# Decoder layer on one core: gathers of the expert blocks released one by one, the token picks looked up six blocks earlier, part of the last weighing and normalising moved

## What is computed

```python
logits = flat @ gate_w.T
probs = softmax(logits)
_, top_idx = top_k(logits + expert_bias, 2)
top_w = take_along_axis(probs, top_idx); top_w = top_w / top_w.sum(-1)
out = sum_e combine[:, e] * swiglu(flat, w_gate[e], w_up[e], w_down[e])    # 16 experts, width 176
out = out + swiglu(flat, sw_gate, sw_up, sw_down)                          # shared expert
x = layernorm(x + out)
```

## Time and profile before

| | us |
|---|---|
| median of 3 runs | 665.21 (661.70 to 668.49) |
| the profiled execution | 668.49 |
| its span | 666.7 |
| TensorE busy | 634.4 (95%) |
| expert blocks, first gate_up to last down | about 577 to 649 |
| rows of the routed experts, weighing, last norm | about 638 to 666.7 |

### The profile page before, as it was taken

How to read it: one execution, slowest core, us unless ns; L and a number is a source line. 1 busy time by engine, 2 the same in 40 slices (tenths; PEclk the granted TensorE clock), 3 DMA queues, 4 the chain that set the end, 5 groups by cost and what they waited for, 6 DMA issues and landing times.

```text
span 666.7 us, 12041 instructions
## 1 busy us (share of the span) xinstructions
PE 634.4 (95%) x3545; PEld 493.7 (74%) x3545; DVE 532.3 (80%) x852; ACT 455.3 (68%) x742; POOL 476.4 (71%) x456
## 2 busy tenths in 40 slices
PE   7989999999999999999999999999999999899980
PEld 6677888878888888788888887878888877555540
DVE  6999999999999999999999999958952646522345
ACT  3768788797887978878879788776423454433454
POOL 4295989879888798798987987596924644855454
PEclk9989999999999999999999999999999988999995
DMA  4261112111131121211311212042063493368444
GB/s 161 83 257 50 64 49 111 63 48 63 48 111 63 48 92 55 74 63 48 111 63 48 69 50 103 0 128 101 16 161 86 111 301 151 110 184 273 124 116 147
DMA packets 25994, 66.67 MB, mean 100 GB/s; under 512 B 4099, under 2 KB 16899, under 8 KB 23179
## 3 DMA queue, kind: packets, MB, share of 16 engines
q1 hardware_dynamic: 23131, 58.54, 26.1%
q0 software_dynamic: 2832, 7.75, 4.5%
HBM read 58.00 MB, written 9.85 MB: 102 GB/s over the span
## 4 chain that ended last, share of the span: by engine, by line
PE 82%; DVE 7%; ACT 3%; POOL 3%; issue 3%; DMA 2%; SPq 0%; ACTq 0%; DVEq 0%
PE ps L878 37%; PE ps L892 9%; PE ps L908 7%; PE ps L893 4%; PE ps L1172 4%; PE ps L810 3%; PE ps L828 3%; DVE conv L1727 3%; PE ps L1221 3%; PE ps L852 2%; DMA xb<-x_scratch,y_all 1%; PE ps L917 1%; PE ps L918 1%; POOL conv L668 1%; PE ps L1146 1%
## 5 line engine op out<-in xcount | busy, mean ns | idle before, releaser
L1727 DVE SCALAR_TENSOR_TENSOR conv<-ps,w_raw,conv 128x506 f32<-128x506 f32 (+3 forms) x352 | 320.7, 934 | 15.9 <-ACT conv L1372 9.9
L878 PE MATMUL ps<-x_hi,w_hi 128*128 128x512 f32 x384 | 158.7, 413 | 3.2 <-DVE x_lo L1648 2.1
L1372 ACT ACTIVATE conv<-ps,w_raw 128x512 f32<-128x512 f32 x160 | 108.2, 687 | 66.0 <-PE ps L878 65.5
L878 PE MATMUL ps<-x_hi,w_lo 128*128 128x512 f32 x384 | 151.6, 395 | 0.0
L878 PE MATMUL ps<-x_lo,w_hi 128*128 128x512 f32 x384 | 150.4, 392 | 0.0
L525 POOL TENSOR_TENSOR decay<-cum_b,cum_tok 128x512 f32<-128x512 f32 (+1 forms) x128 | 103.3, 828 | 8.9 <-DMA cum_b<-cum_scratch 8.9
L878 PEld LDWEIGHTS ps<-x_hi,w_hi 128*128 128x128 f32 x384 | 72.6, 189 | 21.2 <-issue 2.4
L531 POOL TENSOR_TENSOR decay<-decay,mask 128x512 f32<-128x512 f32 x64 | 82.7, 1292 | 5.0
L878 PEld LDWEIGHTS ps<-x_hi,w_lo 128*128 128x128 f32 x384 | 72.3, 188 | 17.0 <-DVE w_lo L1653 0.2
L878 PEld LDWEIGHTS ps<-x_lo,w_hi 128*128 128x128 f32 x384 | 72.7, 189 | 12.7
L1357 ACT ACTIVATE conv<-conv 128x1024 f32<-128x1024 f32 x80 | 79.3, 1059 | 1.5 <-DVE conv L1727 1.5
(11 more groups left out here) (285 smaller groups left out, 1109.8 us busy)
## 6 DMA issues: line engine op xcount, KB each, us to landing
cum_b<-cum_scratch SPq DMA_DIRECT2D x16, 1024.0 KB, 4.6
w_raw<-in_winT SPq DMA_DIRECT2D x15, 778.0 KB, 4.2
y_all<-in_wgu SPq DMA_DIRECT2D x4, 1408.0 KB, 11.9
late<-in_wdn SPq DMA_DIRECT2D x2, 1408.0 KB
x_scratch<-conv SPq DMA_DIRECT2D x19, 128.0 KB, 4.9
late<-in_woutT SPq DMA_DIRECT2D x1, 2048.0 KB, 8.2
ys_scratch<-y_blk SPq DMA_DIRECT2D x32, 64.0 KB
res_scratch<-conv SPq DMA_DIRECT2D x11, 130.0 KB
```

The costliest lines, as they stand in the source:

```text
L878: mm = pe.matmul(ps[:, tile_bank(n, tile) + hf, :], wp[:, par, w], xp[:, kk, t], start=(i == 0), stop=(i == 5))
L1372: act.activation(conv[:, par, tile, hf * 512:(hf + 1) * 512], ps[:, tile_bank(n, tile) + hf, :], ACT.Copy, scale=w_raw[:, par, tap:tap + 1 ...
L1727: dve.scalar_tensor_tensor(out=o[:, :, s:], in0=u[:, :, 0:T - s], scalar=w_raw[:, par, c:c + 1], in1=o[:, :, s:], op0=ALU.mult, op1=ALU.ad ...
```

## The change

`AHEAD` goes from 4 to 3, and each gather_block(j) with j of 3 or more waits for `tx_done` of block j-3, that is for the transpose that read the rows three blocks earlier. The pairs are gone: gather_res(b) follows gather_block(7+b) directly, with a wait on `gu_done` of the last shared item ahead of the first. `SEEN_AT` goes to item 22 (block 11), `PICK_AT` to item 25 (block 14). `beside_blocks` now spaces all rows: rows 0 and 1 wait for gate_up of block 19, rows 2 and 3 of block 20, rows 4 and 5 of block 21, rows 6 to 8 of block 22, rows 9 to 11 of block 23, rows 12 to 15 for down(33). VectorE does weigh_low of output blocks 0 to 2 ahead of gate_block(33) and weigh_high of blocks 0 and 1 ahead of gate_block(34). The last norm is done by ScalarE for blocks 0 to 3, by GpSimd for blocks 4 and 5 (after its last row gather), and by VectorE for blocks 6 and 7 after all weighing.

```diff
-SEEN_AT = TBS + 17
-PICK_AT = TBS + 18
-LAST_ACT = 5
+SEEN_AT = TBS + 11
+PICK_AT = TBS + 14
+LAST_ACT, LAST_POOL = 4, 6
+BESIDE = 19
-AHEAD = 4
+AHEAD = 3
@@ SP, output stores
                 if b < LAST_ACT:
                     sp.wait_ge(S["n2a"], b + 1)
+                elif b < LAST_POOL:
+                    sp.wait_ge(S["n2p"], b - LAST_ACT + 1)
                 else:
-                    sp.wait_ge(S["n2"], b - LAST_ACT + 1)
+                    sp.wait_ge(S["n2"], b - LAST_POOL + 1)
@@ POOL
             def gather_block(j):
+                if j >= AHEAD:
+                    pool.wait_ge(S["tx_done"], j - AHEAD + 1)
                 pool.indirect_dma_start(xb[:, j % NX, :], None, x2_dram,
...
                 if b == 0:
                     pool.wait_ge(S["st_res"], 16 * TBS)
+                    pool.wait_ge(S["gu_done"], TBS)
...
-            for j in range(AHEAD):
+            for j in range(NBLK):
                 gather_block(j)
                 if j == 2:
                     gate_shared(TBS - 1)
                     add_residual(TBS - 5)
                 elif j == 3:
                     add_residual(TBS - 4)
-            for j in range(AHEAD, NBLK, 2):
-                i = TBS + j - AHEAD
-                in_pair(i, 0)
-                gather_block(j)
-                if j == AHEAD:
+                elif j == 4:
                     add_residual(TBS - 3)
-                elif j // 2 - AHEAD // 2 <= TB:
-                    in_pair(i, 1)
-                    gather_res(j // 2 - AHEAD // 2 - 1)
-                in_pair(i, 2)
-                gather_block(j + 1)
-                if j == AHEAD:
+                elif j == 5:
                     add_residual(TBS - 2)
                     add_residual(TBS - 1)
+                if 7 <= j < 7 + TB:
+                    gather_res(j - 7)
             def beside_blocks(n):
-                if n < 6:
-                    in_pair(ITEMS - AHEAD + n // 3 * 2, n % 3)
+                j = BESIDE + min(n // 2, (n + 3) // 3)
+                if j < NBLK:
+                    pool.wait_ge(S["gu_done"], TBS + j + 1)
+                else:
+                    pool.wait_ge(S["dn_done"], ITEMS - 1)
...
+            for b in range(LAST_ACT, LAST_POOL):
+                pool.wait_ge(S["q2"], b + 1)
+                pool.tensor_scalar(o_tok[:, b, :], y_of[:, 0, b, :], ln_m2[:, b, 0:1], ln_v2[:, 1, b:b + 1],
+                                   ALU.subtract, ALU.mult).then_inc(S["n2p"], 1)
@@ DVE
             for i in range(TBS, ITEMS):
+                if i == ITEMS - 2:
+                    for b in range(HOISTED):
+                        weigh_low(b)
+                if i == ITEMS - 1:
+                    for b in range(LEADING):
+                        weigh_high(b)
                 gate_block(i)
...
-            for b in range(HOISTED):
-                weigh_low(b)
-            for b in range(LEADING):
-                weigh_high(b)
             for b in range(HOISTED, TB):
                 weigh_low(b)
             for b in range(LEADING, TB):
                 weigh_high(b)
-                if b > LAST_ACT:
-                    last_norm(b - 1)
-            last_norm(TB - 1)
+            for b in range(LAST_POOL, TB):
+                last_norm(b)
```

More of the change, by code:

```diff
@@ L274, in build_layer @@
                  "ld_sh ld_gu ld_dn ld_copy st_x2 st_res ld_res a_el "
-                 "tx_done a_xt gu_done a_s a_u p_h v_h ht_done a_ht v_ht dn_done a_y p_res v_mix st_out y_seen v_blk v_lb ys_set n2a")
+                 "tx_done a_xt gu_done a_s a_u p_h v_h ht_done a_ht v_ht dn_done a_y p_res v_mix st_out y_seen v_blk v_lb ys_set n2a n2p")
         S = {n: sem(n) for n in names.split()}
```

## The result

| | before | after |
|---|---|---|
| median, same chip, nine runs each | 662.57 us (660.66 to 668.49) | 667.59 us (665.45 to 669.90) |
| after to before | | 1.0066, 95% interval 1.0038 to 1.0095 |
| profiled execution, its span | 668.49, 666.7 | 666.86, 665.1 |

So the change costs 0.66% here, 4 to 5 us; 659.8 was forecast. The two profiled executions hide it: that of before was the slowest of its nine, and its first gather of a block starts at 573.17 us, that of after at 566.72. From there the end is 93.5 us away before (666.7 less 573.17) and 98.4 after: 4.9 more.

A forecast was written before the change was run, and what follows sets the result against it. TensorE was taken to bound the block loop, then POOL's row gathers the end. Span 666.7 less 661.35 gave 5.35 us, 1.0 from the loop; from 665.21 the same 5.4 led to 659.8, range 655.5 to 666.0.

The forecast's parts named there:

- AHEAD in the context FFN: Context FFN: position 3 gains a wait for two transposed blocks, already there in time; cost 0.
- Gathers behind tx_done: Block loop: gather(j) may start after turn_block(j-3), removing the loss at block 13; -0.63 us, bounds 0 and -0.8.
- Picks looked up earlier: Block loop, items 30 to 32: wait of 0.56 us shrinks to 0.2; -0.36 us, up to +1.5 if landing is late.
- Rows started earlier: POOL's row gathers: row 5 issued at 641.1, not 645.94; row 15 at 653.75, 5.0 us ahead.
- Weighing inside the loop: VectorE ahead of gate_block(33) and gate_block(34): the latter 0.9 us late, but covered.
- The last norm: Program's end: GpSimd norms blocks 4 and 5, 1.22 us each, delaying the output stores; costs 0.3 us.
- The base: Whole kernel: median of before taken as 665.21 us, from three runs of 661.7 to 668.49.
- (c): Blocks 6 to 23: gathers right behind turn_block cost 0.43 us per block; 2.3 slower, 667.5 us; chance 0.12.
- (a): Rows held by data, not POOL: stores land in 5 us, row 5 1.9 later; 661.7 us; chance 0.18 with (d).
- (d): Early look at the picks stalls VectorE, landing after 613.4: up to +1.5, 661.3 us; chance 0.18 with (a).

The follow-up runs named there:

- Loop alone: Kernel before with after's gathers, gather_res, AHEAD and early look at the picks, but before's tail: 661.29, 661.68, 660.95, 661.26 and 662.11 us in five runs.
- tail alone: Kernel before with after's rows, weighing, last norm and stores, but before's paired gathers, AHEAD 4 and late look at the picks: 662.71 us, ratio 1.0011.
- the kernel with the late look and no norm on GpSimd: After with gather_res in every other block only, look at the picks at items 28 and 29, no norm on GpSimd: 660.50 and 660.41 us.

## Why the prediction was wrong, step by step

After's end is 10.2 us later than forecast (98.4 against 88.2 from the first gather). The steps that failed are two. The sum has no term for late semaphores of TensorE, and the stalls that they make are 8.2 of it (98.4 against 90.2 on the clean occasion). And it prices the last norm on GpSimd at 0.3, which is the other 2.0 (90.2 against 88.2). The starts of the last gate_up and of rows 5 and 15 came out within 0.4 on a clean occasion; the base, from three runs, was 2.6 too high.

From the first gather of a block, in us. "Clean" is after on its third occasion; the last column is after without GpSimd's norms (its second run).

| | before | forecast | after | after, clean | no norm |
|---|---|---|---|---|---|
| last gate_up starts | 70.2 | 69.2 | 72.5 | 69.3 | 69.8 |
| row 5 starts | 72.8 | 67.9 | 70.8 | 67.5 | 68.0 |
| row 15 starts | 85.6 | 80.6 | 85.0 | 80.4 | 80.9 |
| end | 93.5 | 88.2 | 98.4 | 90.2 | 89.2 |

- **AHEAD in the context FFN**: cost 0, as forecast; the gathers go out 1.25 us apart in after too.
- **Gathers behind tx_done**: right on a clean occasion. Where before waits for gather(13) the period is 2.79 and not 3.42: the 0.63 are gained. They depend on the landing: without the norm, in its second run, gather(14) took 7.3 us to land, and a period there is 2.94. On an occasion with stalls this part was never run alone.
- **Picks looked up earlier**: right in place and nearly in size. The two periods with the table loads (2.90 and 3.36 before) became 2.90 and 3.10: 0.26 gained, 0.36 forecast.
- **Rows started earlier**: right to 0.4 us on a clean occasion. It needs both halves of the change. Loop alone starts row 0 at 62.3 to 65.2, tail alone at 64.25, both together at 60.4. Loop alone gains 0.6 to 1.9 us in five timings; the kernel with the late look and no norm on GpSimd gains 2.3 in two; tail alone gains nothing, but its norms are on GpSimd and cost it time at the barrier; everything but the norms gains 4.2 and 5.2.
- **Weighing inside the loop**: covered, as forecast; the last periods are 2.79 and 2.55 as before.
- **The last norm**: this step failed, and would have on any occasion. "So this costs 0.3" counted the stores alone. GpSimd is not through when its last instruction ends. Its DRAIN at the barrier ends 4.90 to 4.92 us later in all twenty traces, whether that last instruction is a norm, a small sum or the issue of a row's gather, and ScalarE's and VectorE's 0.03 to 0.05 later. In before GpSimd's last gather ends at 659.74 and its DRAIN at 664.64, ahead of SP, which comes to the barrier at 666.5; so it is hidden. With the norm the DRAIN is last, and the span ends 5.15 us behind the norm in after, in both repeats of it and in the tail alone. With the norm SP waits 2.2 us at the barrier; without it, 0.2. In time: 659.51 against 657.47 on the same occasion, 2.0 us; with stalls 667.27 against 663.36, 3.9 us, two small sums standing in for the norms. The contention with VectorE, which the Trainium skill's rule made me weigh (GPSIMD Engine Reference, section 8), cost little: of the eleven norms on GpSimd in these traces ten took 1.22 to 1.24 us, two of these in the tail alone while VectorE ran weigh_highs, and one 1.43, beside a weigh_high in the clean after. The sums of the earlier trace rows agree with the rule better: four ran beside operations of VectorE with two inputs in SBUF and took 0.90 to 1.17 us, the other seven 0.72 to 0.74.
- **A term that was not there**: the stalls. They add 3.2 us up to the last gate_up (72.5 against 69.3) and 8.4 up to where ScalarE takes the last block's result (84.0 against 75.6); after takes 667.3 with them and 659.5 without on the same chip. The forecast put TensorE's signals at 0.3 us from the end of a gate_up to the issue that waits for it, at all times. Nothing in the profile of before told of stalls, though its trace was itself of the sort with events missing: its wait rows put to "issue" what in clean traces has a named releaser. Why an occasion has them stays open.
- **The base.** The median of before was taken as 665.21 from three runs; it is 662.6 to 662.9 in every later set. That the clean after (659.5) lies at the forecast 659.8 is chance: the gain was 3.2 and not 5.4, and the base 2.6 too high. Without the norm, 5.4 was nearly right: 4.2 and 5.2.
- **The rivals.** (c) came to 667.5, the time measured, but not by its mechanism: no block loses 0.43 us to the gather's place, on a clean occasion all keep 2.79, and on the others the time goes in a few stops of 2 to 4 us. (a) did not happen: row 5 starts where forecast. (d) happened in part: on the clean occasion after's VectorE waited 0.72 us for the last gather_res and no gate_up moved, but in the loop alone's fourth run VectorE got going 6.7 us behind the issue of that gather, and the period there is 3.36 and not 2.90; without the norm, in its second run, VectorE waited 1.9 us and the period is 3.20.

GpSimd's and SP's DRAIN at the barrier in the clean after (ns, start): 650.1 and 7.2 make 657.3.

```profile
L97 POOLq DRAIN  x1: 7214/7214/7214, 650.1 to 650.1; - x1
...
L97 SPq DRAIN  x1: 13/13/13, 655.3 to 655.3; - x1
```

The same in the second run without GpSimd's norms, where GpSimd is through at 653.8, ahead of SP:

```profile
L97 POOLq DRAIN  x1: 12436/12436/12436, 641.4 to 641.4; - x1
...
L97 SPq DRAIN  x1: 13/13/13, 655.8 to 655.8; - x1
```

VectorE's wait for the last gather_res, in the timeline of the clean after:

```profile
607.08 0.17 DVE L2039 CAST y_all<-conv 128x16 int32<-128x16 f32 x1 [0.72 <-DMA conv<-res_scratch,cum_b]
```

And why the norm is better with VectorE: in the first run without GpSimd's norms it does all four in 1.37 us, between 650.23 and 651.60, and SP waits 0.2 us at the barrier. Its timeline and SP's waits:

```profile
650.23 1.37 DVE L1823 TENSOR_SCALAR conv<-conv,cum_b 128x256 f32<-128x256 f32 x4
```

```profile
SPq L97 <- PEq L97: 0.2, 1, 0.2
```

## What to carry to other kernels

Don't give GpSimd the last piece of work: count what an engine still needs at the barrier behind its last instruction, here 4.9 us on GpSimd and 0.05 on VectorE, and let something else end later than that. Of this change, keep everything but the norm on GpSimd: 657.5 and 658.7 us against 662.7 and 662.9 on clean occasions. On one with stalls, where it was run with two small sums added, nothing is gained: 663.4 against 662.6. Run a variant beside the unchanged kernel, on more than one occasion, before a loss is put down to an edit: eight runs on two occasions made a clean story here (four edits without stalls, four with) that a repeat of the same texts undid.

## What the runs showed of the hardware

- On some occasions TensorE's semaphore updates reach the other engines late, by 2.5 to 3.2 us at the worst, several together, while its matmuls go on as far as they may; on clean ones they are at most 0.05 us late. Those of ScalarE, VectorE and GpSimd are never over 0.02 us late. The granted clock over the span was 0.985 with the stalls and 0.987 without. A program can be immune (before, 662.6) or lose 8 us (after) on such an occasion. Two occasions on one chip differed, so it isn't the chip alone. Dense indirect DMAs (two in each period of 2.79 us, then rows) mark the kernels that were hit, and within their traces the stretches with late updates; but this is only a coincidence in time: no kernel with fewer of them but before itself ran on such an occasion, and what differs between occasions no run here shows.
- On those occasions the trace lacks about a thousand of 6,200 semaphore updates, nine in ten of them of landing DMAs, so that waits get the releaser "issue" or "remote". The number of updates in a trace tells how far its named releasers can be trusted.
- GpSimd's DRAIN at the program's last barrier ends 4.90 to 4.92 us after its last instruction in all twenty traces, be it a norm, a small sum or the issue of an indirect DMA; ScalarE's and VectorE's 0.03 to 0.05 after theirs. No kernel without indirect DMAs was run, so whether they are the reason isn't shown.
